# The products of the exponentials with V in pairs, the sums of the step ahead in front of them, in a two-layer attention kernel

## What is computed

```python
# layer 0, per batch and head
q = softmax(q, axis=-1);  k = softmax(k, axis=1)
att = einsum('bnhd,bnhl->bhdl', k, v)
y   = einsum('bnhd,bhdl->bnhl', q, att)
# layer 1
att = softmax(einsum('bnhl,bmhl->bnmh', q, k) + (1 - mask) * -1e6, axis=2)
y   = einsum('bnmh,bmhl->bnhl', att, v)
# both
out = x + silu(layer_norm(y) * (1 + scale) + shift) @ W_out + b_out
```

## Time and profile before

| | before |
|---|---|
| runs (us) | 1452.62, 1458.72, 1458.91; median 1458.72 |
| profiled execution's own time | 1455.05 us, of it span 1453.2 us |
| TensorE busy | 1366.8 us, 94% of the span |
| DVE, ACT, POOL busy | 69%, 56%, 53% |
| mean granted TensorE clock | 0.98 |

### The profile page before, as it was taken

How to read it: one execution, slowest core, us unless ns; L and a number is a source line. 1 busy time by engine, 2 the same in 40 slices (tenths; PEclk the granted TensorE clock), 3 DMA queues, 4 the chain that set the end, 5 groups by cost and what they waited for, 6 DMA issues and landing times.

```text
span 1453.2 us, 20521 instructions
## 1 busy us (share of the span) xinstructions
PE 1366.8 (94%) x7040; PEld 965.2 (66%) x7040; DVE 998.9 (69%) x1958; ACT 809.8 (56%) x1417; POOL 772.4 (53%) x692
## 2 busy tenths in 40 slices
PE   6899999999999799999999999998999999999985
PEld 4688888888888675566665665665665666566543
DVE  5787887878879676657647746756655656746754
ACT  4454455455455535656647646746745755665562
POOL 0323343243333425558658667566666756846952
PEclk9999999999999899999999999999999999999997
DMA  9011121111222266546336336335434643633520
GB/s 329 28 39 58 37 94 46 50 63 33 95 80 81 73 204 222 163 140 187 102 118 200 119 116 186 121 109 185 135 117 136 177 124 117 181 117 108 167 74 30
DMA packets 82888, 172.93 MB, mean 119 GB/s; under 512 B 7240, under 2 KB 7240, under 8 KB 82784
## 3 DMA queue, kind: packets, MB, share of 16 engines
q1 hardware_dynamic: 82784, 171.62, 38.3%
HBM read 104.45 MB, written 67.14 MB: 118 GB/s over the span
## 4 chain that ended last, share of the span: by engine, by line
PE 72%; DVE 12%; DMA 5%; ACT 5%; POOL 2%; issue 2%; SPq 1%; POOLq 0%; DVEq 0%; ACTq 0%
PE ps L497 14%; PE ps L499 13%; PE ps L498 13%; PE ps L653 7%; PE ps L687 7%; PE ps L670 7%; PE ps L492 5%; DVE cT L1183 5%; DMA Ks<-mask_scratch 4%; PE ps L708 2%; PE ps L606 1%; ACT xTh L768 1%; ACT ps L770 1%; PE ps L585 1%; DVE ps L1154 1%
## 5 line engine op out<-in xcount | busy, mean ns | idle before, releaser
L1345 POOL TENSOR_TENSOR Pb<-Pb 128x512 f32<-128x512 f32 x376 | 471.6, 1289 | 207.2 <-PE ps L687 171.8
L907 ACT ACTIVATE Pb<-ps 128x512 f32<-128x512 f32 x512 | 278.9, 610 | 212.2 <-PE ps L670 153.8
L1183 DVE TENSOR_REDUCE cT<-ps 128x1 f32<-128x512 f32 x512 | 327.3, 683 | 98.0 <-PE ps L653 97.9
L653 PE MATMUL ps<-Ks,Qs 98*128 98x512 f32 x512 | 190.0, 414 | 11.3 <-DMA Ks<-mask_scratch 7.2
L670 PE MATMUL ps<-Qs,Ks 106*128 106x512 f32 x512 | 187.7, 414 | 2.1 <-DVE xTl L1042 1.7
L653 PEld LDWEIGHTS ps<-Ks,Qs 98*128 98x128 f32 x512 | 92.7, 188 | 83.8 <-DVE cT L1183 34.2
L670 PEld LDWEIGHTS ps<-Qs,Ks 106*128 106x128 f32 x512 | 95.0, 189 | 57.3 <-DVE cT L1183 16.4
L1269 POOL TENSOR_TENSOR rs<-ve,mhalf 128x4 f32<-128x4 f32 x32 | 33.0, 1032 | 180.8 <-DVE ve L1015 134.1
L1297 POOL TENSOR_TENSOR vt<-vt,qmx 128x512 f32<-128x512 f32 x32 | 33.7, 1055 | 163.0 <-DVE qmx L1107 163.0
L497 PE MATMUL ps<-xTh,Wh_k 128*128 128x512 f32 x256 | 109.7, 429 | 4.7 <-DVE xTl L1042 3.6
L497 PE MATMUL ps<-Wh_o,sTh 128*128 128x512 f32 x256 | 107.3, 419 | 2.8 <-DVE sTl L1162 2.8
(11 more groups left out here) (175 smaller groups left out, 2940.6 us busy)
## 6 DMA issues: line engine op xcount, KB each, us to landing
Qs<-stack_scratch SPq DMA_DIRECT2D x32, 768.0 KB
Ks<-stack_scratch SPq DMA_DIRECT2D x32, 768.0 KB
stack_scratch<-sg_q SPq DMA_DIRECT2D x32, 512.0 KB, 2.7
stack_scratch<-sg_k SPq DMA_DIRECT2D x32, 512.0 KB, 2.6
wr<-in_x SPq DMA_DIRECT2D x32, 256.0 KB, 4.5
x_scratch<-wr SPq DMA_DIRECT2D x32, 256.0 KB, 2.0
stack_scratch<-sg_q SPq DMA_DIRECT2D x32, 256.0 KB, 2.9
stack_scratch<-sg_k SPq DMA_DIRECT2D x32, 256.0 KB, 3.3
```

The costliest lines, as they stand in the source:

```text
L653: e.matmul(bank[:], Qs[par][0:RX, j, t * 128:(t + 1) * 128], Ks[par][0:RX, j, :], start=True, stop=True).then_inc(s["S"], 1)
L907: e.activation(p_buf(n, m)[:, j, :], ps[bank_of["a", n, m, j]][:], ACT.Exp).then_inc(s["P"], 1)
L1183: e.tensor_reduce(nx[:, n % 2, j, t, 0:1], ps[bank_of["S", n, j, t]][:], AX.X, ALU.max, negate=True).then_inc(s["S_max"], 1)
L1345: e.tensor_tensor(acc[:, j, :], acc[:, j, :], p_buf(n, m)[:, j, :], ALU.add).then_inc(s["Ps_pool"], 1)
```

## The change

It does four things:
1. The parts `("pv", n, m)` are now only `m` = 0 and 2, and each issues the products of two tiles, m and m + 1, directly behind each other. Each tile still waits for its own four exponentials.
2. The denominator product leaves `tl` and becomes a part `den`. For steps with g = 1, 2, 3 the products of the first pair call it with n - 1, so it stands directly in front of them. For g = 0 it is a part of the track `tlx`, and after the last step it stands in the tail.
3. The pairs have a track of their own (`pv` in `PLAN`), apart from the score products (`att`).
4. `COST` of a pair is 2.0, where two single ones were 1.1 each; that of `den` is 0.9 where it was 1.1. All marks of layer 1 are new, and some of layer 0.

The number of matmuls, exponentials, additions and DMAs stays what it was. The operands, buffers and banks are the same. In the changed file the lines of TensorE before `pv` are 5 lower (L653 is L648, L670 is L665, L497 to L499 are L492 to L494); the products with V are L703 and the denominators L681.

```diff
-    "a": (0.216,), "pv": (1.1,), "ae": (0.0,),
-    "tl": (0.2, 0.1, 0.9, 1.1), "tlx": (1.0, 0.0, 0.4, 0.4, 0.4, 0.4),
+    "a": (0.216,), "pv": (2.0,), "den": (0.9,), "ae": (0.0,),
+    "tl": (0.2, 0.1, 0.9), "tlx": (1.0, 0.0, 0.4, 0.4, 0.4, 0.4),
...
+    "pv": ((0.38, 0.768, 0.868), (0.337, 0.76, 0.879), (0.489, 0.956, 1.054), (0.328, 0.759, 0.832)),
...
-    "0v": ((0.56, 1.051), (0, 0.565)),
+    "0v": ((0.691, 1.2), (0, 0.565)),
...
-        att = []
-        for m in range(NT + 1):
-            if m < NT:
-                att += [("a", n, m, j) for j in X]
-            if m:
-                att += [("pv", n, m - 1)]
-        att += [("ae", n)]
...
-        put("att", att)
+        put("att", [("a", n, m, j) for m in range(NT) for j in X])
+        put("pv", [("pv", n, 0), ("pv", n, 2), ("ae", n)])
...
-            put("tlx", [("tl", n - 1), ("tlx", b - 1), ("ny", 8 + b - 1)])
+            put("tlx", [("tl", n - 1), ("den", n - 1), ("tlx", b - 1), ("ny", 8 + b - 1)])
...
+            def pv(i, n, first):
...
+                b, g = divmod(n, NG)
+                if first == 0 and g:
+                    den(0, n - 1)
+                for m in (first, first + 1):
+                    e.wait_ge(s["P"], 16 * n + 4 * m + 4)
```

More of the change, by code:

```diff
@@ L179, in the_order @@
         weave(o, *tracks)
-    weave(o, ([("tl", N1 - 1), ("tlx", B - 1), ("ny", 15)] + [("ty", 15, c) for c in range(5)] + tiles("o", 15), 0, 1))
+    weave(o, ([("tl", N1 - 1), ("den", N1 - 1), ("tlx", B - 1), ("ny", 15)] + [("ty", 15, c) for c in range(5)] + tiles("o", 15), 0, 1))
     o.append((("end",), 0))
@@ L671, in a, with den @@
                          start=True, stop=True).then_inc(s["ST"], 1)
-            def pv(i, n, m):
+            def den(i, n):
                 b, g = divmod(n, NG)
[L675 to L684, removed]
-                for j in range(4):
[L686 to L689, removed]
+                pool, dve = ps_count(n, 3, 3)
+                e.wait_ge(s["Ps_pool"], pool)
+                if dve:
+                    e.wait_ge(s["Ps_dve"], dve)
+                if n == 0:
+                    e.wait_ge(s["sel"], 2)
+                    if bank_before["bank", 7] is not None:
+                        e.wait_ge(*done(bank_before["bank", 7]))
+                elif g == 0:
+                    e.wait_ge(s["rd"], b)
+                for j in range(4):
+                    r = e.matmul(DEN[32 * j:32 * j + 32, :], sel[:, 4 - g:36 - g], p_buf(n, 0)[:, j, :],
+                                 start=(g == 0), stop=(g == NG - 1))
+                r.then_inc(s["den"], 1)
@@ new lines, in pv @@
+            def pv(i, n, first):
[4 more added lines that the diff above has]
+                    e.wait_ge(s["P"], 16 * n + 4 * m + 4)
+                    if m == 0:
+                        if n == 0:
+                            if bank_before["bank", 6] is not None:
+                                e.wait_ge(*done(bank_before["bank", 6]))
+                        else:
+                            e.wait_ge(s["y1"], n)
+                        if g == 0:
+                            e.wait_ge(s["v_hi"], 4 * (8 + b) + 4)
+                    pb = p_buf(n, m)
+                    for j in range(4):
+                        h = 4 * g + j
+                        r = e.matmul(PV[32 * j:32 * j + 32, :], xbuf(8 + b)[:, m, h * 32:(h + 1) * 32], pb[:, j, :],
+                                     start=(m == 0), stop=(m == NT - 1))
+                    r.then_inc(s["PV"], 1)
@@ L695, in tl @@
                     turn(PV, [yt[:, t * 128:(t + 1) * 128] for t in range(NT)]).then_inc(s["y1_tr"], 1)
[L696 to L710, removed]
             def tlx(i, b):
@@ L717, in _ @@
             parts = {"m": m, "mb": mb, "tx": tx, "k": k, "v": v, "te": te, "q": q, "st": state, "y": y, "ty": ty, "o": o,
-                     "qk": qk, "S": S, "nxt": nxt, "a": a, "pv": pv, "tl": tl, "tlx": tlx}
+                     "qk": qk, "S": S, "nxt": nxt, "a": a, "pv": pv, "den": den, "tl": tl, "tlx": tlx}
             for p, i in order:
```

22 lines of the change are left out of this document (11 added, 11 removed), and 8 rows, old and new, of the table PLAN.

## The result

The changed kernel takes 1436.29 us (median of 4 runs, 1434.84 to 1439.45) beside 1458.82 us for the kernel before on the same chip: ratio 0.9862, 95% interval 0.9844 to 0.9879, so faster by 1.4%. The profiled execution took 1437.03 us.

A forecast was written before the change was run, and what follows sets the result against it. TensorE, busy 94% of the span, was taken as the bound. Joins -29 us, layer 0 +1, tail +1 and late exponentials +1 sum to -26 us; set between 1432.7 (median) and 1429 (profile): 1431 us, range 1417 to 1447 us.

The forecast's parts named there:

- The joins: Products with V and denominators on TensorE: 87 more joins, each saving 0.33 us (0.19 shape changes, 0.14 overlap), 29 us.
- The triple: Sign in steps with g = 1: denominator and two tiles' products start 0.86 us apart, the whole row 2.7 us.
- The rival in which a join saves only the changes of shape: Joined products on TensorE: 0.19 us saved per join, 16.5 us in all, giving 1442 to 1444 us; chance 0.05.
- A batch: Sign in layer 1: the window over one batch is about 109 us long, with TensorE busy some 105 us.
- First and second pair at 0: Pairs of each layer 1 step: no new waits for exponentials, taken as 0; without cover up to 1 us per first pair.
- The denominator as cover: First pair: denominator and tile 0's product ahead give tile 1's exponentials about 1.0 us of slack.
- The sign that was set, under 3 us for `Pb` of ACT in sum: Profile after: TensorE's waits for ACT's exponentials (`Pb`) should stay under 3 us in sum.
- Maxima kept at 2 us a batch: TensorE's wait for carried maxima, once a batch in layer 1: kept at 2 us, 1 us either way (8 us).
- The clock, a rival at 0.05: Low clock stretches behind the maxima wait vanish in eight batches, gaining 14 us more: 1417 us; chance 0.05.
- Layer 0 at +1: Layer 0, no slack on TensorE: later transposes and queued low parts on VectorE cost 1 us, bounds 0 and 5.
- The tail at +1: From 1403 us on: joins save less and tile 2's score products come behind the first pair, 1 us more.
- +1 for late exponentials: Single exponentials that come late for TensorE: about 1 us more in all.

The follow-up runs named there:

- e4: The kernel before with tile 0's product with V issued twice, directly behind each other, in each of 32 steps: 1480.8 us, ratio 1.016.
- e3: The changed kernel with the denominator on its own track a few matmuls ahead of the first pair, 64 joins left of 88: 1446.75 us, ratio 0.9922.
- e2: The changed kernel with its marks, but each tile's product with V a part of its own again, 48 joins left of 88: 1453.71 us, ratio 0.9985.
- e1: The kernel before with its old marks, products with V issued in pairs, denominators left in place, 65 joins: 1516.36 us, ratio 1.0405.
- e8: The changed kernel with the carried maxima of steps with g = 0 moved earlier (marks 0.74, 0.87): 1441.47 us, ratio 0.9918.
- e9: The changed kernel with only the q mark of steps with g = 2 moved later, from 0.021 to 0.2: 1454.67 us, ratio 0.9981.
- after_again: The changed kernel, unaltered, measured and profiled a second time: 1439.27 us, ratio 0.9869 to the kernel before.

## Why the prediction was right, and where its sum was off

**The joins: right, mechanism and size.** The triple takes 2.72 us where 2.7 was forecast. In e4 a joined product adds 0.86 us; in e3 24 joins are worth 8.7 us, in e2 40 of them some 17. The rival in which a join saves only the changes of shape is out, by the starts. The count was off by one: before, the last step's products of tiles 2 and 3 also stood next to each other, with a wait of 1.58 us between them, so 86 joins are new. The Trainium skill, "TensorE: Matmul & The Clock Gate", section on packing small matmuls, lets a weight load overlap matmuls in flight only when the row group differs. All rows are in use here, and by that rule a joined product would take the 1.00 us of a single one, as an estimate. The runs show 0.86, so here the measurement decides against the rule.

**A batch: right.** 108.7 us with TensorE busy for 105.4, where 109 and 105 were forecast.

**First and second pair at 0: right in the middle, with a condition.** TensorE waits 1.3 us for exponentials in six batches, and never inside a pair. e1 shows what the term was worth had the pairs stood elsewhere: 28 us of waits for `Pb` in six batches. The denominator as cover wasn't needed: in e3 tile 1's product stands 1.2 us behind that tile's last score product in the steps with g = 1, against 2.1 us in the changed kernel, and `Pb` still costs only 0.4 us of waits. The sign that was set, under 3 us for `Pb` of ACT in sum, failed over the whole of layer 1: 5.2 us, of which 2.6 stand ahead of the last step's tiles 2 and 3.

**Maxima kept at 2 us a batch: wrong by 1.5 us a batch.** They fell to 0.5, 8.8 us in six batches, just beyond the bound of 8 that I had set for all eight. I had counted the 4 us of work that now lies ahead of that place, and let the closer packing of the 16 products cancel it. At that place it did not. The packing costs at another, inside the row of these products, which now stall for DVE's reductions without being printed (777.70 above).

**The clock, a rival at 0.05: happened in part.** The six batches of the kernel before hold five low stretches, near 676, 789, 901, 1014 and 1113 us, 1.7 us lost in each and 8.5 in sum; the first profile of the changed kernel has none there, the second has one. The first batch kept its 0.97. A step that I had not linked: four of the five stood behind the wait for the maxima, the fifth behind a wait of 2.1 us for a load. The other kernels go along: no low stretch behind waits of 0.5 us at that place (changed kernel) and 0.7 us (e8), low stretches again behind waits of 1.5 us at another place (e9) and of 1.76 us at a third, where 1.40 us left the clock alone (`after_again`). But it isn't the wait alone: the last two of the six waits of some 1.95 us before were followed by no low stretch, nor was one of 2.15 us in `after_again`. That is a correlation; no run changed one wait and left the rest. Over the whole program the second profile of the changed kernel loses as much to low stretches as the kernel before, 29 us, since it has more of them in layer 0 and behind the last batch.

**What took it back.** In the six batches 66 joins are 22 us, the clock 8.5, and all printed waits, the maxima among them, are 5.7 us less: 36 us in sum, and 23.8 were measured. That leaves some 12 us. The count of the waits bears on it: 40 instead of 26, and at 802.50 a wait lost 0.27 us beyond the idle that is printed; 14 x 0.27 = 4 us, as an estimate. The rest are mostly stops too short to be printed. Counted by the starts in the two traces, outside the changes of shape, 32 products of the changed kernel that wait for DVE or ACT without a printed idle start 7.5 us later in sum than the 0.23 us pitch has it; 17 of them, with 5.2 us, wait for the reductions of the products for the maxima. Before there are 7, with 0.3 us. That leaves about 1 us open, and the closer packing pays back a good part of what the shorter wait for the maxima brought.

**The ends: mis-sized.** Layer 0 at +1 came out at -1 by the first profile and at +4 by the second. The two differ by their low stretches, which cost 5.1 and 10.2 us up to the first product with V (6.8 before), so the size of this term isn't shown. The tail at +1, with +1 for late exponentials, measured +3.6 in the last batch and +1.7 behind it, by the second profile +1.1 and +1.3. Denominator and tile 3's product of the last step wait some 1.6 and 2.1 us in both, and the denominator behind them (in the first profile tile 3's product too) took 1.94 us instead of 1.06, at the low clock. The first profile has a stacked load that waits 2.0 us besides, with a low stretch behind it. The first batch, with no term of its own beside its joins, lost 1.5 us by the first profile and gained 0.6 by the second, although it has 11 joins, 3.6 us; why is open. Outside the six batches the sum had 21 joins, 7 us, against 3 us of costs, so -4 us; by either profile it was some +6 us. That 10 us is the whole miss of the first profile (-18 where -26 was forecast), since the middle was 2 us better: 22 us of joins forecast, 23.8 measured. That the middle came out so close was luck: two errors nearly cancelled there, the maxima and the clock for the better and the many small waits for the worse, some 17 us each way, and none of them stood in the sum. By the medians the gain is 22.5 us, and 1436.3 lies 5 us above 1431, inside the range.

## What to carry over

Price a matmul of few columns by starts, not by durations: here the changes of shape (0.19 us) and the end that doesn't overlap (0.14 us) were paid once a row, so groups of the same shape were worth putting together where TensorE was the bound. The order around them decides the sign: pairs under the old marks cost 4% where the second tile's exponentials were late. Take a second profile of the same kernel before a few us in one stretch are explained. After such a change look for the longest wait that is left and move one mark at a time; of two marks moved together here, one gained 0.65% and the other lost 1.1%.

## What the hardware did that I had not expected

- Groups of 32 columns that stand behind each other start 0.86 us apart, 0.14 us less than the 1.00 us of a single one, with all rows in use, and the weight loads of the second start at 1405.86 while the first is printed as running until 1406.49.
- A wait of TensorE can cost more than its length. Behind some waits of 1.5 us and more the clock was 0.66 over 5 us (and 940 to 945 us in e9), which costs about 1.7 us, as much as the wait. In the six middle batches of the fourteen profiles all 40 low stretches stand at or right behind a wait of 1.5 us or more, 14 other waits of that length have none behind them, and no shorter wait has one.
- The printed idle understates a stall: 0.21 us shown, 0.48 us lost at 802.50, and nothing shown for the 0.92 us lost from 777.70 to 779.55.
